# Mixing of the FFN's folded weights over tiles: every second pair on ScalarE and GpSimd instead of VectorE

## The reference

```python
def butterfly(y, weights, dim):             # weights: (10 stages, 512, 2, 2), dim = 1024
    for stage in range(weights.shape[0]):
        s = 2 ** stage
        nb = dim // (2 * s)
        yr = y.reshape(*lead, nb, 2, s)
        a, b = yr[..., 0, :], yr[..., 1, :]
        w = weights[stage].reshape(nb, s, 2, 2)
        na  = w[..., 0, 0] * a + w[..., 0, 1] * b
        nb2 = w[..., 1, 0] * a + w[..., 1, 1] * b
        y = jnp.stack([na, nb2], axis=-2).reshape(*lead, dim)
    return y

h = x @ W_exp + b_exp                       # 256 -> 1024
h = butterfly(h, up_weights, 1024)
h = gelu(h + up_bias)
h = butterfly(h, down_weights, 1024)
y = h @ W_con + b_con + down_bias           # 1024 -> 256
```

## Time and profile before

| | us |
|---|---|
| median of 3 runs | 1158.23 |
| lowest and highest | 1155.43, 1165.39 |
| the profiled execution | 1159.59 |
| its span | 1157.7 |

### The profile page before, as it was taken

One profiled execution on the slowest core, in us unless ns is written; L12 is line 12 of the kernel. 1 busy time (PEld: TensorE's weight loads), 2 busy tenths in 40 slices (PEclk: granted clock), 3 DMA queues, 4 the chain that ended last, 5 costly groups with the idle time before them and its releaser, 6 DMA issues.

```text
span 1157.7 us, 28789 instructions
## 1 busy us (share of the span) xinstructions
PE 1061.5 (92%) x8974; PEld 786.9 (68%) x8974; DVE 874.8 (76%) x1948; ACT 722.3 (62%) x1113; POOL 569.0 (49%) x565
## 2 busy tenths in 40 slices
PE   5678889999999999999999999999999999988876
PEld 4464557767677776768677777768677776757575
DVE  6679967787877878787877878787877878777354
ACT  2176649474776749475776749475776749474523
POOL 2443526455472836455472836455472836443311
PEclk8688889999999999999999999999999999998999
DMA  7765554646465564646465564646465564641111
GB/s 279 158 204 122 168 120 132 176 104 204 105 194 128 186 164 132 183 111 202 104 195 126 186 165 130 186 110 202 101 196 128 175 176 133 181 112 50 66 38 37
DMA packets 94984, 169.91 MB, mean 147 GB/s; under 512 B 14872, under 2 KB 36120, under 8 KB 94944
## 3 DMA queue, kind: packets, MB, share of 16 engines
q1 hardware_dynamic: 93888, 166.53, 52.6%
q10 hardware_dynamic: 832, 1.83, 0.4%
q0 software_dynamic: 224, 1.04, 0.2%
HBM read 92.28 MB, written 77.07 MB: 146 GB/s over the span
## 4 chain that ended last, share of the span: by engine, by line
PE 62%; DVE 16%; ACT 10%; issue 6%; DMA 4%; POOL 1%; SPq 1%; ACTq 0%; DVEq 0%; POOLq 0%
PE ps_m L639 20%; PE ps_m L765 10%; PE ps_m L799 7%; PE ps_m L693 6%; PE ps_m L774 5%; PE ps_m L804 4%; DVE m_raw L1001 4%; PE ps_t L736 4%; DVE g_lo L481 4%; ACT pT L874 3%; PE ps_m L722 2%; ACT gact L950 2%; DVE x1T L1046 2%; DMA m_scr<-small 1%; ACT L874 1%
## 5 line engine op out<-in xcount | busy, mean ns | idle before, releaser
L874 ACT ACTIVATE pT<-ps_t 128x512 f32<-128x512 f32 x640 | 330.0, 603 | 255.6 <-PE ps_t L736 255.3
L1168 POOL TENSOR_SCALAR_AFFINE_SELECT pT<-pT 128x512 f32<-128x512 f32 (+1 forms) x320 | 193.0, 608 | 382.1 <-ACT pT L874 379.9
L1001 DVE TENSOR_REDUCE m_raw<-ps_m 128x1 f32<-128x512 f32 (+2 forms) x768 | 338.1, 501 | 23.2 <-PE ps_m L722 22.1
L693 PE MATMUL ps_m<-k_st,q_st 48*128 48x512 f32 (+3 forms) x1024 | 154.9, 358 | 36.9 <-DMA k_st<-qk_scr 7.2
L765 PE MATMUL ps_m<-pT,v_aug 128*32 128x512 f32 (+3 forms) x2048 | 156.4, 447 | 7.3 <-DVE m_raw L1001 3.2
L639 PE MATMUL ps_m<-x1T,w_hi 128*128 128x512 f32 x512 | 152.0, 404 | 1.6 <-ACT x1T L906 1.0
L693 PEld LDWEIGHTS ps_m<-k_st,q_st 48*128 48x128 f32 x1024 | 88.1, 190 | 96.2 <-issue 47.5
L736 PE MATMUL ps_t<-q_st,k_st 50*128 50x512 f32 (+3 forms) x1024 | 124.5, 350 | 4.5 <-DMA q_st<-m_scr 3.1
L765 PEld LDWEIGHTS ps_m<-pT,v_aug 128*32 128x32 f32 x2048 | 59.1, 112 | 87.0 <-issue 78.7
L639 PEld LDWEIGHTS ps_m<-x1T,w_hi 128*128 128x128 f32 x512 | 94.4, 189 | 25.9 <-issue 2.2
L804 PE MATMUL ps_m<-w_hi,g_lo 128*128 128x256 f32 x512 | 83.6, 286 | 6.8 <-DVE g_lo L481 6.7
(11 more groups left out here) (122 smaller groups left out, 2095.4 us busy)
## 6 DMA issues: line engine op xcount, KB each, us to landing
qk_scr<-rot_hi SPq DMA_DIRECT2D x62, 512.0 KB, 4.7
q_st<-qk_scr SPq DMA_DIRECT2D x128, 192.0 KB, 4.3
k_st<-qk_scr SPq DMA_DIRECT2D x128, 192.0 KB, 4.7
qk_scr<-rot SPq DMA_DIRECT2D x32, 512.0 KB, 5.3
o_scr<-o_raw SPq DMA_DIRECT2D x64, 256.0 KB, 3.6
r_b<-in_xT SPq DMA_DIRECT2D x17, 512.0 KB, 5.1
o_c<-o_scr SPq DMA_DIRECT2D x32, 256.0 KB
r_b<-r_scr SPq DMA_DIRECT2D x32, 256.0 KB
```

The source lines that it names most:

```text
L693: return pe.matmul(scores[r][:, off:off + (qt + 1) * P], q_st[rows, pr, qt * P:(qt + 1) * P], k_st[rows, pr, 0:(qt + 1) * P], start=start, ...
L874: act.activation(pT[:, slot, half * T:(half + 1) * T], ps_t[:, ST_BANK[2 * n + r], :], ACT.Exp, scale=SCALE).then_inc(exp_done, 1)
L1001: ins = dve.tensor_reduce(m_raw[:, g % 2, r, u // 2, qt:qt + 1], scores[:, off:off + (qt + 1) * P], AX.X, ALU.max, negate=True)
L1168: pool.affine_select(out=v, in_=v, compare_op=ALU.is_ge, fill=0.0, base=0, pattern=pattern, channel_multiplier=-1).then_inc(mask_done, 1)
```

## The change

Pairs with an even n stay as they are. For a pair with an odd n, ACT makes the two products across as before, waits for its own two products (it is about to overwrite the tiles that they read), and then scales both tiles in place by their own weights; POOL adds `tmp_x` to each. DVE does nothing for it. The semaphore `bx` is split into one for DVE's pairs and one for POOL's; whoever waited for all pairs now waits for both. `pair_products(n)` counts ACT's signals.

```diff
+        def pair_products(n):
+            return n + 1 + (n + 1) // 2
...
                     if n > 1:
-                        act.wait_ge(bx[k], 2 * (n - 1))
+                        wait(act, bx[0][k], 2 * (n // 2))
+                        wait(act, bx[1][k], 2 * ((n - 1) // 2))
                     elif k:
                         act.wait_ge(wz_in, DMA)
-                        act.wait_ge(bx[0], 2 * (11 + n))
+                        act.wait_ge(bx[0][0], 12)
+                        act.wait_ge(bx[1][0], 12)
...
                     for x, tile in enumerate((second, first)):
-                        act.activation(tmp_x[:, n % 2, x, :], tile, ACT.Copy,
-                                       scale=w_x[:, k, st, 1 + x, p:p + 1]).then_inc(bt[k], 1)
+                        ins = act.activation(tmp_x[:, n % 2, x, :], tile, ACT.Copy,
+                                             scale=w_x[:, k, st, 1 + x, p:p + 1])
+                    if n % 2:
+                        ins.then_inc(bt[k], 1)
+                        act.wait_ge(bt[k], pair_products(n) - 1)
+                        for x, tile in enumerate((first, second)):
+                            ins = act.activation(tile, tile, ACT.Copy, scale=w_x[:, k, st, 3 * x, p:p + 1])
+                    ins.then_inc(bt[k], 1)
...
-                elif kind in ("XU", "XD"):
+                elif kind in ("XU", "XD") and n % 2 == 0:
...
-                    dve.wait_ge(bt[k], 2 * (n + 1))
+                    dve.wait_ge(bt[k], pair_products(n))
...
+                elif kind in ("XU", "XD") and n % 2:
+                    k = int(kind == "XD")
+                    first, second, _, _ = pair((tile_up, tile_dn)[k], k, n)
+                    pool.wait_ge(bt[k], pair_products(n))
+                    for x, tile in enumerate((first, second)):
+                        pool.tensor_tensor(tile, tile, tmp_x[:, n % 2, x, :], ALU.add).then_inc(bx[1][k], 1)
```

More of the change, by code:

```diff
@@ L431, in layer @@
         bf = [sem("up_stage"), sem("down_stage")]
-        bx = [sem("up_cross"), sem("down_cross")]
+        bx = [[sem("up_cross"), sem("down_cross")], [sem("up_cross_pool"), sem("down_cross_pool")]]
         bt = [sem("up_products"), sem("down_products")]
@@ L822, in one @@
                     if n == 0:
-                        pe.wait_ge(bx[0], 12 * 2)
+                        pe.wait_ge(bx[0][0], 12)
+                        pe.wait_ge(bx[1][0], 12)
                     k, half = n // 2, n % 2
@@ L832, in one @@
                         pe.wait_ge(bf[1], STAGES_IN - 1)
-                        pe.wait_ge(bx[1], 12 * 2)
+                        pe.wait_ge(bx[0][1], 12)
+                        pe.wait_ge(bx[1][1], 12)
                     pe.matmul(pm[:, 0:D], mat[1][-1][:, n * P:(n + 1) * P], tile_dn[n],
@@ L954, in one @@
                     if isinstance(b, int) and (b, n) == (0, 0):
-                        act.wait_ge(bx[1], 12 * 2)
+                        act.wait_ge(bx[0][1], 12)
+                        act.wait_ge(bx[1][1], 12)
                     wait(act, done["W2"], NT * b)
@@ L1114, in one @@
                                                  in1=tmp_x[:, n % 2, x, :], op0=ALU.mult, op1=ALU.add)\
-                           .then_inc(bx[k], 1)
+                           .then_inc(bx[0][k], 1)
                 elif kind == "XB":
```

## The result

| | before | changed |
|---|---|---|
| median, us | 1159.46 (8 runs) | 1168.01 (8 runs) |
| lowest and highest | 1155.43, 1165.39 | 1166.05, 1175.6 |
| ratio to before, 95% interval | | 1.0068, 1.0044 to 1.0091 |
| measured again on another occasion | 1159.94 (35 runs) | 1165.31 (12 runs), 1.0051, 1.0029 to 1.0073 |

A forecast was written before the change was run, and what follows sets the result against it. DVE was taken to bound the stretch from 71.4 to 155 us. Its saving of 9.9 us, 9.5 us of new idle time and 2.1 us for `rstd` gave net +1.7 and 1160 us, range 1151 to 1169 (own range 1156 to 1164).

The forecast's parts named there:

- three places in the queues: Late exponentials delay DVE's (0, 8) reduction 2.7 us; `UT` behind additions delays `w_lo` 4.8; `rstd` behind additions costs 2.1.
- the lateness is kept: Rival: `w_lo`'s 4.8 us not won back in (1, 0), slower rounds into (1, 3), (1, 4), `rstd`: +9.4 us, 1167.6; chance 0.15.
- The bound: From 71.4 to 155 us DVE, busy 79.0 of 83.6 us, bounds; time taken off it can count in full.
- the round is hidden: Rival: PE's and DVE's queues bear the late exponentials, DVE's saving comes through, 1148.3 down to 1144.7 us; chance 0.14.
- The price of the operations: ACT's 24 scalings 0.42 us each, 10.2 in all; its own wait 0.1; POOL's additions 1.35 a pair, 16.2 in all.
- The round: Closed loop from one step's exponentials through masks, POOL's additions and ACT's products and scalings to the next: 5.9 us a step.
- From the late exponentials to VectorE: In (0, 8) DVE's reduction starts at 99.4 instead of 96.70, 2.7 us late; about 1 to 2 us late at (0, 9).
- `w_lo`: Behind `UT` and late exponentials of (1, 0), DVE's `w_lo` starts at 117 instead of 112.15, 4.8 us late.
- The term that failed, the collision: In (1, 0) DVE's mixing falls from 3.84 to 0.8 us, 3.0 back, as the collision with POOL's subtraction goes.
- `rstd`: On POOL behind the last pair's additions, at 153.7 instead of 151.98; normalisation 1.7 us late; +2.1 us by queue position.
- The sum: Whole kernel: -9.9 us of DVE's work, +9.5 of new DVE idle time, +2.1 by `rstd`'s position: net +1.7 us.
- one of the bad cases: Slower by more than 1%, some 11.6 us, was said to need two bad cases together; chance 0.06.

The follow-up runs named there:

- the best complete version: Changed kernel with POOL's additions ahead of the masks, up pair 11 and down pairs 1 and 11 left on VectorE: 1156.4 us, ratio 0.9974 to the kernel before.

## Why the forecast was right, and where its size was off

The direction and the three places in the queues were right. The number was not: 1160 was forecast with a range of its own of 1156 to 1164, and 1168.0 and 1165.3 lie above that. They lie within 1151 to 1169 because the range was widened for the rival "the lateness is kept", and the first of them only just. That part is luck.

**The bound.** I read from 79.0 busy of 83.6 us that a microsecond off VectorE counts in full. With nothing in its place 11.9 us less work on VectorE shortened the stretch by 6.3, and without the additions the time fell by 6.5. This didn't touch my sum, which spent the saving on new waits, but no run came near the rival "the round is hidden" at 1144.7 to 1148.3, though two of them left work out, and the best complete version stops at 1156.4.

**The price of the operations.** ScalarE's scalings, 0.42 us each, held: a group of two takes 0.91 with its end. The wait for its own result, put at 0.1, cost 0.1. GpSimd's pair of additions was 1.35 and measured 1.41.

**The round.** 5.9 us forecast, 5.97 measured, three times in a row. With the order alone changed, the round and the loss are both gone.

**From the late exponentials to VectorE.** The conclusion held, its row did not. I took the reduction at 96.70 for the one behind the exponentials. By its form it is the step's first `S`, which stands ahead of `ST`; the one that waits is the next, at 97.90 before and at 100.99 in the changed kernel, with 1.85 us of idle time ahead. From the start of the stretch it is 2.0 us late; I had said 2.7. The row was the wrong one, so it is partly luck that the two lie near each other. But by (0, 9) VectorE was 3.1 us late, not 1 to 2, since GpSimd's additions now fell onto its last pair and onto four small products of the bias, which took 1.34 us.

**`w_lo`.** 4.8 us late forecast, 5.6 measured from the start of the stretch; 3.21 us idle ahead.

**The term that failed, the collision.** "What DVE gets back is its mixing in (1, 0): 0.8 us instead of 3.84 [...] since the collision with POOL's subtraction goes (POOL comes to it later)". It measured 2.98, and 2.97 to 3.00 in every other version with two fused operations there: VectorE comes later by as much, so the collision stays. VectorE left (1, 0) 4.4 us late instead of 1.8. This is the 2.2 us collision that I named as the first part of the rival "the lateness is kept". From there to `WO` I had it win back 2.2 us; it won 0.9 (3.5 us late at the first `WO` sum).

**`rstd`.** 2.1 us forecast, 2.0 measured between the `WO` sum and the normalisation, of which 1.5 to 1.7 went when the pair was taken out of its way.

**The sum.** +1.7 forecast, +6.1 on the stretch. The measured +6.1 is 3.5 at the `WO` sum, 1.9 more by the start of the `PV` group behind `rstd`, and 0.7 in that group, which ran at a lower granted clock than before (0.53 against 0.64). Of the clock the prediction had said that its rows say nothing, and it put it at nothing. The 4.4 us that the forecast lacks are the collision with 2.2, less won back behind it with 1.3, the later `w_lo` with 0.8, and the clock with 0.7, less 0.6 in small terms.

The rival "the lateness is kept", 1167.6, had 0.15 of the chances. Its own sign was that VectorE's idle time grows by more than the 9.9 us that it is spared. It grew by 10.2 us over the 92 us from the stretch's start (92 less 82.0 busy before, less 71.9 now), and by 12.3 over 71.4 to 155. So what happened is nearer to this rival than to the forecast, though not in all of its parts: its steps of 6.9 and 6.3 us into (1, 3) and (1, 4) took 7.2 and 6.9, and the exponentials of (1, 4) were 7.7 us late where I had said 4.1, but VectorE bore it: it was 4.4 us late behind (1, 0) and 3.5 at `WO`. That the move would stay within 1% was right: one of the bad cases came, and not two. That a measurement can't tell less than 1% was wrong: the interval of the ratio reaches 0.24% to either side.

**The rule that I weighed.** It speaks as the runs do. The four tiny products on `setup`, two SBUF inputs each, took 1.34 us where they took 0.37 before, while GpSimd was adding. The Trainium skill, "SBUF — State Buffer", section "Who interferes with whom", has the shared ports as an exclusive lock: whoever issues first holds them for its whole instruction, and the other is blocked. The prediction priced the collisions with the new additions at 1.35 us a pair, as a rival, and took the old one with the subtraction to be gone; the old one stayed, with 2.2 us.

## What to carry to other kernels

Work moved to an idle engine is priced by its place in that engine's queue, not by its duration: ask what the instructions ahead of it wait for, and what stands behind it. Here the same additions cost 12 to 14 us behind two masks and 3 to 6 ahead of them. And before an engine is relieved, leave the work out once: here 12 us less on the busiest engine gave about 6, and no way of moving the work that I tried gave more than about 3.

## What the runs showed of the hardware

- A collision isn't shared out by number: four fused operations (1.65 us alone) beside one subtraction took 3.84 us, and two of them (0.82 alone) beside the same subtraction took 2.98 and 2.99. Both times it is 2.2 us more, near the 2.38 us of the subtraction, however few the short ones are.
- ScalarE's wait for its own result costs about 0.1 us: products end at 78.71 by the record, the scaling that waits for them starts at 78.73, where operations without a wait start 0.09 us before the record ahead ends.
- The same `PV` group took 2.36 us at a granted clock of 1.00 (2.4 GHz), 3.66 at 0.64 before and 4.40 at 0.53 in the changed kernel. Over 92 us the mean granted clock was 0.85 in both kernels without additions and 0.78 to 0.83 in all the others, in no order with the length of their stretch.
